# Centring, scaling and splitting the projection biases on GpSimd instead of VectorE in batch 0's opening microseconds

## What is computed

```
x = x + cross_attention(layernorm(x), context)
x = x + ffn(layernorm(x))

q    = ln_head(xn @ Wq + bq)                     # 16 heads of 32
k, v = ln_head(ctx @ Wk + bk), ctx @ Wv + bv     # 496 positions
kd   = ln_head(ctx_dca @ Wkv_dca + bkv_dca)[k]   # 16 positions, with vd beside it
out  = (softmax(q k^T / sqrt(32)) v + softmax(q kd^T / sqrt(32)) vd) @ Wo + bo

ffn(x): lut[gate_idx], lut[up_idx], lut[down_idx] are the weights (1376 wide); silu(gate) * up, then down
```

## Time and profile before

| | before |
|---|---|
| median of 3 runs | 806.87 us |
| the profiled execution | 806.87 us |
| its span, first to last instruction | 805.1 us |
| PE busy | 757.8 us (94%) |
| DVE busy | 513.0 us (64%) |
| ACT busy | 491.7 us (61%) |
| POOL busy | 264.8 us (33%) |

### The profile page before, as it was taken

How to read it: one execution, slowest core, us unless ns; L and a number is a source line. 1 busy time by engine, 2 the same in 40 slices (tenths; PEclk the granted TensorE clock), 3 DMA queues, 4 the chain that set the end, 5 groups by cost and what they waited for, 6 DMA issues and landing times.

```text
span 805.1 us, 14839 instructions
## 1 busy us (share of the span) xinstructions
PE 757.8 (94%) x5833; PEld 310.6 (39%) x5833; DVE 513.0 (64%) x991; ACT 491.7 (61%) x1001; POOL 264.8 (33%) x276
## 2 busy tenths in 40 slices
PE   2888786999999999999999999999999999999998
PEld 1342232333443343324443342235433433365445
DVE  7979999898877994225769953228499800153211
ACT  3479889788646886662658866636488855511100
POOL 6883221000763321113843321035622210014320
PEclk9998999899999999999999999999999999999999
DMA  7749997586430001221500003222000000100001
GB/s 255 195 126 268 259 259 214 140 188 156 125 81 1 1 2 33 74 53 59 122 6 1 2 15 78 54 66 54 2 1 1 1 28 27 41 14 1 0 14 40
DMA packets 74389, 61.49 MB, mean 76 GB/s; under 512 B 33424, under 2 KB 60816, under 8 KB 74064
## 3 DMA queue, kind: packets, MB, share of 16 engines
q1 hardware_dynamic: 73984, 60.29, 28.2%
q10 hardware_dynamic: 208, 0.26, 0.1%
q0 software_dynamic: 128, 0.00, 0.0%
HBM read 43.55 MB, written 10.55 MB: 67 GB/s over the span
## 4 chain that ended last, share of the span: by engine, by line
PE 77%; DVE 13%; ACT 3%; POOL 3%; issue 3%; DVEq 0%; POOLq 0%; ACTq 0%
PE ps L1699 51%; PE ps L2050 8%; PE ps L2031 6%; PE ps L2002 5%; PE ps L1750 5%; DVE arena L1141 4%; DVE nmax L1494 3%; POOL hrstd L701 2%; PE ps L2037 2%; ACT ps L1024 2%; PE ps L1898 2%; DVE nmax L1499 1%; DVE stat L1178 1%; DVE arena L1148 1%; POOL xrstd L645 1%
## 5 line engine op out<-in xcount | busy, mean ns | idle before, releaser
L1699 PE MATMUL ps<-arena,wf_hi 128*128 128x512 f16 (+2 forms) x736 | 211.0, 371 | 0.7 <-issue 0.7
L1024 ACT ACTIVATE ps<-ps,nmax 128x496 f32<-128x496 f32 x256 | 166.1, 652 | 23.3 <-DVE nmax L1499 23.3
L1056 ACT ACTIVATE arena<-ps 128x1024 f32<-128x1024 f32 x128 | 124.3, 1026 | 72.1 <-PE ps L2037 72.1
L1699 PE MATMUL ps<-arena,wf_lo 128*128 128x512 f16 (+2 forms) x368 | 136.1, 370 | 0.0
L1699 PE MATMUL ps<-wf_hi,arena 128*128 128x512 f16 (+3 forms) x374 | 114.8, 368 | 0.5 <-DVE arena L1148 0.2
L701 POOL TENSOR_TENSOR hrstd<-hvar,mhalf 128x16 f32<-128x16 f32 (+1 forms) x33 | 100.8, 3068 | 39.5 <-DVE hvar L1248 39.4
L1699 PEld LDWEIGHTS ps<-arena,wf_hi 128*128 128x128 f16 (+1 forms) x736 | 69.5, 100 | 85.8 <-issue 21.5
L1141 DVE TENSOR_SCALAR arena<-arena,wf_lo 128x2048 f16<-128x2048 f16 (+1 forms) x132 | 89.5, 739 | 5.6 <-PE ps L1750 5.4
L1750 PE MATMUL ps<-arena,wf_lo 128*32 128x512 f16 (+1 forms) x1056 | 66.4, 396 | 13.5 <-ACT arena L851 9.5
L645 POOL TENSOR_TENSOR xrstd<-xvar,mhalf 128x1 f32<-128x1 f32 x32 | 23.8, 743 | 158.5 <-DVE xvar L1183 158.5
L1699 PE MATMUL ps<-wf_lo,arena 128*128 128x512 f16 (+3 forms) x187 | 68.5, 366 | 0.0
(11 more groups left out here) (154 smaller groups left out, 1049.1 us busy)
## 6 DMA issues: line engine op xcount, KB each, us to landing
arena<-idx SPq DMA_DIRECT2D x124, 128.0 KB, 3.6
arena<-in_x SPq DMA_DIRECT2D x32, 256.0 KB, 2.9
wf_lo<-in_idx SPq DMA_DIRECT2D x10, 512.0 KB, 5.3
idx<-wf_hi SPq DMA_DIRECT2D x10, 384.0 KB, 4.4
out<-arena SPq DMA_DIRECT2D x15, 256.0 KB, 2.1
wf_lo<-in_idx SPq DMA_DIRECT2D x11, 256.0 KB, 6.8
arena<-in_ctxT SPq DMA_DIRECT2D x5, 512.0 KB, 3.8
v_next<-arena SPq DMA_DIRECT2D x8, 256.0 KB, 4.5
```

What stands on the lines that cost most here:

```text
L1024: last = act.activation(sc, sc, ACT.Exp, bias=nmax[:, 0, t, h:h + 1], accum_out=den[:, 0, t, h:h + 1])
L1056: act.activation(probs[n_ % 2][:, 2 * p:2 * p + 2, :], ps[:, bank:bank + 2, :], ACT.Exp).then_inc(s["probs_set"], 1)
L1699: last = pe.matmul(dst, l, r, start=(first and i == 0), stop=(stop and i == len(todo) - 1))
```

## The change

GpSimd takes over `bias_centre` and `bias_low`. VectorE keeps the sums (`bias_sums`). On GpSimd the centring is three instructions instead of one: scale the 64x16 sums by WS/32, scale the whole 128x512 bias tile by WS, and subtract with the sums spread over each head. Since the tile is now already scaled, ScalarE's high half loses its factor. The low half is then a plain subtraction, in two instructions of 32x512, the second waiting for the first. GpSimd does the centring behind `shift_patterns`, ahead of `norm(1, 2)`, and the low halves between `norm(1, 2)` and `norm(1, 3)`.

```
@@ GpSimd @@
+            def bias_centre():
+                pool.wait_ge(s["b_sum"], 1)
+                b_ = st_b[0:64, :].rearrange("p (h d) -> p h d", d=HD)
+                link(pool.tensor_scalar(sum_b[0:64, :], sum_b[0:64, :], WS / HD, 0.0, ALU.mult, ALU.add))
+                link(pool.tensor_scalar(st_b, st_b, WS, 0.0, ALU.mult, ALU.add))
+                pool.tensor_tensor(b_, b_, sum_b[0:64, :].unsqueeze(2).to_broadcast([64, H, HD]), ALU.subtract).then_inc(s["b_cent"], 1)
+
+            def bias_low():
+                pool.wait_ge(s["b_hi"], 1)
+                pool.wait_ge(s["rstd1"], 3)
+                for i, lo in enumerate((32, 96)):
+                    rows_ = slice(lo, lo + 32)
+                    pool.tensor_tensor(b16[rows_, :], st_b[rows_, :], b16[rows_, :], ALU.subtract).then_inc(s["b_lo"], 1)
+                    pool.wait_ge(s["b_lo"], i + 1)
...
             shift_patterns()
+            bias_centre()
             norm(1, 2, (0, 0))
+            bias_low()
             norm(1, 3, (0, 0))
@@ ScalarE @@
-                    act.activation(b16[:, :], st_b, ACT.Copy, scale=WS).then_inc(s["b_hi"], 1)
+                    act.activation(b16[:, :], st_b, ACT.Copy).then_inc(s["b_hi"], 1)
@@ VectorE @@
                     standardise(1, 1, a, x_first[1], x_first[1])
-                    bias_centre()
                     query_centre(3)
...
                     query_low(2)
-                    bias_low()
                     query_low(3)
...
-            def bias_centre():
-                dve.wait_ge(s["b_sum"], 1)
-                dve.scalar_tensor_tensor(out=heads(st_b[0:64, :]), in0=spread(sum_b[0:64, :]), scalar=-1.0 / HD, in1=heads(st_b[0:64, :]),
-                                         op0=ALU.mult, op1=ALU.add).then_inc(s["b_cent"], 1)
-
-            def bias_low():
-                dve.wait_ge(s["b_hi"], 1)
-                for lo in (32, 96):
-                    rows_ = slice(lo, lo + 32)
-                    low(b16[rows_, :], st_b[rows_, :], b16[rows_, :]).then_inc(s["b_lo"], 1)
```

## The result

The change makes the kernel slower: 810.39 us, the median of 12 runs (808.01 to 811.49), against 806.89 us (805.86 to 808.76, 12 runs). The ratio is 1.0043, with a 95% interval of 1.0035 to 1.0051, which is 3.5 us. I had forecast 808.1 with a range up to 809.4, and had given 0.60 to a time between 805.3 and 808.5, no difference to be told. The direction of the likeliest case was right, its size was not, and the time lies near where rival (2) had put it, at 810.2.

A forecast was written before the change was run, and what follows sets the result against it. The opening was taken as a relay bound by VectorE, then GpSimd's powers: 2.03 us removed from VectorE, but key_sums 1.2 us later through ScalarE's delay and held reads, so 806.87 + 1.2 = 808.1 us, range 806.0 to 809.4.

The forecast's parts named there:

- the likeliest case: Opening: VectorE idles for ScalarE's delayed slices, shifting everything after by 1.2 us; 807.4 to 808.8, chance 0.50.
- rival (2): TensorE's second chain of 12 matmuls stays at the slow pace, 2.5 us longer; 810.2, chance 0.12.
- The carrier: Late b_cent releases ScalarE 2.7 us later, delaying Wq's third and fourth slices; VectorE idles 2.7 us behind turn.
- the held reads: VectorE and GpSimd block each other's SBUF reads: query_low(2) held until 20.25, both query_low done at 21.5.
- Rivals (1): GpSimd isn't held out by VectorE or slips in early, b_cent at 16.8 to 17; 806.1 to 806.9, chance 0.26.
- (4): Third slice of Wq leaves ScalarE before the biases, so only VectorE's relief arrives; 804.8, chance 0.03 including the unknown.
- The pace of TensorE: Second chain of 12 matmuls: 0.23 us each before; at 0.43 it would take 2.5 us more.
- the first term: Opening: key_sums on VectorE, then GpSimd's first power and all that follows, come 1.2 us later.
- Rival (3): GpSimd's second bias_low becomes the last wait of project(0), b_lo at about 25; 809.1, chance 0.09.
- The end moves as the first power moves: From rstd(0) on, GpSimd's chain, TensorE's stretch to 53 us and the end shift by the same amount, 1.2 us.

The follow-up runs named there:

- centre_only: Changed kernel with the low halves of the biases given back to VectorE, GpSimd keeping the centring and scaling: 810.27 us, ratio 1.0049.
- hi_later: Changed kernel with ScalarE's high half of the biases moved behind the third and fourth slice of Wq: 806.64 us, ratio 0.9999.
- fill_first: Changed kernel with three extra unused matmuls in the hole of TensorE's first query chain: 810.21 us, ratio 1.0036.
- low_later: Changed kernel with GpSimd's low halves of the biases waiting until VectorE has written all four low halves of Wq: 807.78 us, ratio 1.0017.
- low_only: Changed kernel with the centring given back to VectorE, GpSimd scaling the biases and writing their low halves: 805.70 us, ratio 0.9988.
- fill_both: Changed kernel with extra unused matmuls on TensorE, three inside the first query chain and four between the two chains: 809.07 us, ratio 1.0028.

## Why the prediction was wrong, point by point

**The carrier was read rightly.** That `b_cent` is on the path through ScalarE's program, that a relieved VectorE would stand still behind `turn` (forecast 2.7 us, measured 2.51), that the 64x16 scaling would take 1.7 us (1.64) and end at 16.4 (16.38), and that `b_cent` would come at 18.4 (18.2, because the subtraction took 1.04 us and not 1.15): all of it stands in the rows. `centre_only` and `hi_later` show that this is the cause of the first part of the loss, together with the held reads below. Rivals (1) and (4) are out.

**The sizing of the held reads was short by 0.7 us.** I let GpSimd's first low half hold `query_low(2)` until 20.25 and then gave VectorE both `query_low` in a row, 1.25 us. Measured: the pair ended at 22.21. TensorE's rows give the two ends, since its third slice starts at 20.70 and, after a hole, the fourth at 22.26 (`fill_first` shows the same start in a row of its own). GpSimd's second low half got in between the two, and VectorE waited once for each. The row I had leaned on, the power of the earlier trace rows, was held out through several VectorE instructions back to back; here the GpSimd instruction got its turn when VectorE's first ended, ahead of `query_low(3)`. Why the turn went to GpSimd this time no run tells. So `key_sums` came at 22.12 instead of 21.4, and the first power at 26.76 instead of 26.05: +1.94 for my +1.2. `low_later` shows the whole item, 1.49 us.

**The pace of TensorE was the step that failed.** I had the mechanism, its place and its price as rival (2), and gave it 0.12 and left it outside the range. Its price was good: I wrote 2.1 us beyond the first term, and it was 1.87; I wrote "some 3.9 us" for the second `variance`, and it was 4.68, of which 0.7 is the item above. What was wrong is the chance. I had counted a hole of 1.4 us in the first chain and overlooked in my own timeline that the two chains, 0.90 us apart before, would be 1.3 us apart by my numbers (24.1 to 25.4) and 1.98 in fact. I had also not asked when the rate rose before: the earlier trace rows have the bias matmul still slow at 22.66 (0.63 us) and the next matmul, at 24.19, fast, so the rise lay behind an unbroken first chain, and only just ahead of the second. A hole in that chain could well put it behind the second, so the slow chain was no outside chance and belonged in the range. The runs show both outcomes for idle times of this size, so rows of the kernel before alone could not have settled it. With the two terms as measured, 806.87 + 1.94 + 1.87 = 810.7, against 810.39. That rival (2)'s own 810.2 comes so close is partly luck: its first term was 0.7 us too small, its second 0.2 too large, and the time moved 0.3 less than the marker.

**Rival (3)** didn't occur: `b_lo` came at 21.65, ahead of the bias matmul at 23.51.

**"The end moves as the first power moves"** holds within the scatter only. The marker moved by 3.81 us, the profiled span by 2.9 and the medians by 3.5. From the first matmuls of the scores to the end it was 750.3 us in the profile before and 749.4 after, and between 749.2 and 752.2 in the other profiles, for identical work. What sets that is only in part known (below).

## What to carry to other kernels

Before work is moved off a busy engine, look for who waits for its result and what is queued behind that wait: here a step that took 0.6 us of VectorE's time took from 14.65 to 18.20 us on GpSimd and was done 2.5 us later than before, ScalarE's program passed that on to two slices of Wq that had nothing to do with it, and moving one instruction in ScalarE's order was worth as much as the whole loss. Work for GpSimd that reads SBUF is better placed where VectorE reads PSUM or reduces: in `low_later` the first low half took 1.15 us beside the sums of the keys, and these 1.21 as ever, while the pair of `query_low` beside the same work in the changed kernel took 2.79 for 1.29. And when an edit opens idle time of one or two microseconds on TensorE early in a kernel, price the next group of matmuls at both rates and take the slow one as a case of equal standing.

## What the runs showed of the hardware that I had not expected

**The turns of VectorE and GpSimd.** One GpSimd instruction was held out through VectorE's instructions back to back (the 64x16 scaling, 1.64 us, in every kernel with the centring on GpSimd), and another was let in between two of them (the second low half, 18.94 to 21.65 for two of about 1.1 us). In `hi_later` both engines were in each other's way at once: 2.24 us for VectorE's pair, 1.35 for GpSimd's subtraction. The Trainium skill ("SBUF — State Buffer", section "Who interferes with whom") says that issue order decides who blocks. The rows agree for an instruction that finds the other engine at work, as the 64x16 scaling did at 14.74 us. Which engine gets the next turn when both have work waiting no run here settles.

**32 partitions cost GpSimd as much as 128.** In `low_later` the two low halves of 32x512 took 1.15 us each, as much as 128x512 of the same operation.

**The idle time that makes TensorE slow is no fixed number here.** Second chains behind 0.44 (`low_only`), 0.90, 1.51 and 1.97 us of idle time (`fill_both`) were fast, and so was the one of `low_later`, behind 0.46, 1.52 and 1.29 us around its third slice and its bias matmul. In `hi_later` one behind only 0.49 and 1.29 us was slow for most of its length, and behind 2.83 us in `fill_first` and `centre_only` too. What TensorE did before differs in each, and no rule for it comes out of these runs.

**The rest of the kernel scatters by more than the effects studied.** From the scores' start to the end, the profiled executions took 749.4 to 752.2 us for the same instructions. In one long window of it, 141 to 643 us, VectorE, ScalarE and GpSimd are busy within 2 us of each other in both kernels, and TensorE is not (before, then after; the columns of the earlier trace rows):

```profile
141.00:643.00 502.00, 499.54 (x3866) 198.32 (x3866) 348.35 (x717) 343.86 (x688) 166.16 (x168) 0.99 0.21 53
```

```profile
141.00:643.00 502.00, 495.65 (x3854) 196.96 (x3854) 350.13 (x722) 345.67 (x695) 165.97 (x168) 1.00 0.22 54
```

The windows stand at the same times and, after the shift, not over the same work, so little hangs on these sums. But the clock goes with the scatter. Behind the scores' start the five profiles with 13.7 to 14.0 us at the half level took 749.2 to 750.6 us, and the eight with 17.1 to 17.6 us took 750.0 to 752.2. And of 21 executions of the kernel before on one chip the two with a mean granted clock of 0.994 took 805.5 us on average, the ten with 0.989 took 806.9, the two with 0.987 took 807.6. It is not all of it, since those ten alone lie between 806.45 and 808.32; the rest stays open. This scatter is why medians here resolve no better than 0.1%, where starts inside one execution can be compared to 0.1 us.
